# A graph layer on one core: main path started before its tests are known, lists loaded first, and no filler matmuls

## The reference

```python
msg = node_feat[src] + edge_feat
neigh = segment_sum(msg, dst, num_segments=3125)
rst = (1.0 + eps[0]) * node_feat + neigh
h = rst @ W1 + b1                       # 256 wide
h = (h - mean(h, 0)) * rsqrt(var(h, 0) + 1e-5) * gamma + beta
out = relu(h) @ W2 + b2
result = layernorm(x + out)
```

## Time and profile before

| | us |
|---|---|
| median of 3 runs | 265.76 |
| lowest, highest | 264.14, 265.84 |
| the profiled execution | 265.49 |
| its span, first to last instruction | 263.7 |
| PE, DVE, ACT, POOL busy | 240.7, 187.8, 127.9, 172.6 |

### The profile page before, as it was taken

The page is one execution under the profiler, slowest core; times in us unless marked ns, Lnnn a source line. Parts: engine busy times, 40 slices in busy tenths (PEclk is TensorE's granted clock), DMA queues, the critical chain, the costliest instruction groups (busy, mean ns, idle before and its releaser), DMA issues.

```text
span 263.7 us, 6841 instructions
## 1 busy us (share of the span) xinstructions
PE 240.7 (91%) x2205; PEld 201.5 (76%) x2205; DVE 187.8 (71%) x686; ACT 127.9 (48%) x225; POOL 172.6 (65%) x113
## 2 busy tenths in 40 slices
PE   0649689999999999999999999999999999999980
PEld 0548568889999998788888888878888879845980
DVE  2978894768789986887887878777666511288882
ACT  0406512445565665455645555544444232176794
POOL 3058888888888888888888888888888600270000
PEclk9999956999999999999999999999999999999996
DMA  5975655677789888777888787877776400000034
GB/s 156 271 232 109 138 115 100 151 153 177 192 193 209 189 196 193 171 184 189 200 186 187 183 193 176 192 165 176 156 160 155 81 0 2 4 0 0 2 114 130
DMA packets 48957, 38.11 MB, mean 145 GB/s; under 512 B 5019, under 2 KB 47947, under 8 KB 48921
## 3 DMA queue, kind: packets, MB, share of 16 engines
q1 hardware_dynamic: 32829, 30.62, 40.3%
q0 software_dynamic: 14400, 6.56, 20.8%
q10 hardware_dynamic: 1692, 0.48, 1.0%
HBM read 36.05 MB, written 1.60 MB: 143 GB/s over the span
## 4 chain that ended last, share of the span: by engine, by line
PE 79%; DVE 12%; issue 3%; ACT 2%; DVEq 2%; DMA 1%; ACTq 1%
PE ps L682 28%; PE ps L690 20%; PE ps L720 9%; PE ps L714 7%; PE ps L636 4%; PE ps L781 3%; PE ps L706 2%; DVE hit_k L952 2%; PE ps L770 2%; DVE hit_k L949 2%; DVE aggT L1022 2%; PE ps L711 1%; ACT big L561 1%; DMA x_room<-in_dst_dram 1%; PE ps L619 1%
## 5 line engine op out<-in xcount | busy, mean ns | idle before, releaser
L438 POOL DMA_INDIRECT egat<-in_x_dram,srci x100 | 163.6, 1636 | 43.1 <-issue 28.3
L524 ACT ACTIVATE big<-ps 128x500 f32 x158 | 96.7, 612 | 109.8 <-PE ps L720 83.6
L690 PEld LDWEIGHTS ps<-hit_c,ebuf 128*128 128x128 f32 x632 | 103.2, 195 | 14.9 <-DVE hit_c L920 4.7
L690 PE MATMUL ps<-hit_c,ebuf 128*128 128x20 f32 x632 | 97.3, 232 | 6.4 <-DVE hit_c L920 4.6
L1022 DVE TENSOR_TENSOR aggT<-aggT,ps 128x20 f32 x208 | 35.9, 173 | 54.9 <-PE ps L690 35.5
L682 PE MATMUL ps<-big,xN 128*128 128x114 f16 (+8 forms) x225 | 59.7, 278 | 0.4 <-ACT big L524 0.3
L682 PE MATMUL ps<-big,x_room 128*128 128x114 f16 (+8 forms) x225 | 59.6, 278 | 0.0
L682 PE MATMUL ps<-big,xr 128*128 128x114 f16 (+8 forms) x225 | 59.5, 278 | 0.0
L720 PE MATMUL ps<-hit_k,hit_l 128*128 128x400 f16 x158 | 53.2, 337 | 0.0
L714 PE MATMUL ps<-hit_k,hit_l 128*128 128x300 f16 x158 | 46.5, 294 | 0.0
L952 DVE TENSOR_TENSOR hit_k<-iota_k,key 128x800 f16<-128x800 f16 x79 | 44.9, 568 | 0.0
(11 more groups left out here) (105 smaller groups left out, 209.3 us busy)
## 6 DMA issues: line engine op xcount, KB each, us to landing
ebuf<-in_edge_attr_dram SPq DMA_DIRECT2D x79, 256.0 KB
egat<-in_edge_attr_dram SPq DMA_DIRECT2D x49, 128.0 KB
egat<-in_x_dram,srci POOLq DMA_INDIRECT x100
out_dram<-big SPq DMA_DIRECT2D x5, 256.0 KB
w_sb<-in_L_gnn_W_dram ACTq DMA_DIRECT2D x2, 128.0 KB, 6.9
out_dram<-big SPq DMA_DIRECT2D x2, 128.0 KB
x_room<-in_dst_dram SPq DMA_DIRECT2D x1, 192.0 KB
x_room<-in_src_dram ACTq DMA_DIRECT2D x1, 192.0 KB
```

The lines of the kernel that those rows point to most:

```text
L438: return nc.gpsimd.indirect_dma_start(to, None, x[:, :], bass.IndirectOffsetOnAxis(ap=ix, axis=0), compute_op=op)
L524: nc.scalar.activation(cnt[:, :, bass.ds(lows[m % LOADS], WIN)], ps[:, m % BANKS_C, 0:KEYS].rearrange("p (t n) -> p t n", n=WIN), ACT.Copy ...
L690: last = nc.tensor.matmul(ps[:, SUMS + w % BANKS_S, 0:WIN], rows_v[:, j * D:(j + 1) * D], hits_v, start=(j == 0), stop=(j == ROWS - 1))
```

## The change

- **One path first.** The branch ahead of the loop is gone. The loop always runs; the tests are cut in seven steps that DVE does at windows 21, 24, ... 39 of its loop, PE shares the result behind window 42, the flag is set at index 46, and block 2's multiply waits for it. The branch (`If(flag == 0)`) stands near the end: on ACT ahead of the hidden stores, on DVE ahead of the last sums (with the batch statistics inside), on PE behind four of the eight matmuls on x + b2, on SP and POOL behind their loops. The general path is now the `Else`, loads lists and x again, and does the whole sum anew. `firsts` is clamped (two operations on DVE) so that a wrong input can't write outside.
- **Order of the head.** SP waits for both lists before it issues any edge, then chunks, slots and x in seven pieces by turns, then the weights (from ACT's queue). Key rows come before low bits; rel, sources and carry are copied by ACT; clearing `cnt`'s end is moved ahead of the lists' arrival. The constants made by POOL are smaller.
- **Constants.** `FROM_B` 4 to 5 (counts b 400 to 375 columns, its hit table 400 to 376), the last two blocks (8 and 2 groups) are one of 10, `MARGIN` 36 to 30, x split every third window (`SPREAD`) and transposed two tiles a window (`X_RATE`), `KEEP` 24 to 0. A helper `fill` is there, with all its counts at zero.

By the planner's arithmetic the block sizes were 114, 180, 256, 376, 468, 466, 332, 120, 110 columns, and become 120, 180, 256, 376, 468, 466, 332, 218. The first gathered windows were 6, 9, 12, 14, 18, and become 7, 10, 13, 16, 18. Block 0 is multiplied from window 13 on both before and after.

```diff
-FROM_B = 4
-WIN_B = WIN - FROM_B
+FROM_B = 5
+WIN_B = 15
-BLOCKS_C = (10, 12, 17, 25, 31, 31, 22, 8, 2)
+BLOCKS_C = (10, 12, 17, 25, 31, 31, 22, 10)
-MARGIN = 36
+MARGIN = 30
-SPREAD = 2
-X_RATE = 3
+SPREAD = 3
+X_RATE = 2
-KEEP = 24
-KEEP_FROM = 7
+KEEP = 0
+KEEP_FROM = 0
-KEPT = 810
+KEPT = 0
-TURN = 1660
+TURN = 0
-GATHER_FIRST = 16000
+GATHER_FIRST = 19000
+TEST_STEP = 3
+FILL_HEAD = 0
+FILL_KEY = 0
+FILL_LO = 0
+FILL_CARRY = 0
+FILLS = ()
...
+        LAST_TILE = [max(n for n in range(NT) if X_TILES[n][0] == i) for i in range(NB)]
+        SCALE_AT = [next(m for m in range(GC) if C_AT[m] >= n // X_RATE) for n in LAST_TILE]
+        TEST_F = 1
+        W_TESTS = READY[0] + 8
+        W_WORST = W_TESTS + 7 * TEST_STEP
+        W_SHARED = W_WORST + 4
...
-            for n in range(SLOTS):
+            sp.wait_ge(dst_loaded, 80)
+            sp.wait_ge(src_loaded, 64)
+            chunk(0)
+            x_piece(X_ORDER[0])
+            slot(0)
+            x_piece(X_ORDER[1])
+            chunk(1)
+            x_piece(X_ORDER[2])
+            slot(1)
...
+            chunk(3)
+            x_piece(X_ORDER[6])
+            for n in range(3, SLOTS):
                 slot(n)
-                if n < CHUNKS:
-                    chunk(n)
+            sp.dma_start(w1_sb[:, :], w1).then_inc(weights_loaded, 16)
...
             nc.scalar.activation(srcf, srcq, ACT.Copy).then_inc(src_rows_made, 1)
+            act.wait_ge(rel_turned, 1)
+            nc.scalar.activation(spread(rel[:, :]), banked(2), ACT.Copy).then_inc(rel_made, 1)
...
+            act.wait_ge(src_turned, 1)
+            nc.scalar.activation(spread(srci[:, :]), banked(7)[:, QC:Q, :], ACT.Copy).then_inc(sources_made, 1)
...
+                for i in range(NB):
+                    if SCALE_AT[i] == m:
+                        scale_x(i, x_turned, x_scaled)
...
+                    if u == 0 and f == TEST_F + 1:
+                        pe.wait_ge(path_known, 1)
...
-                    if KEEP_FROM <= m < KEEP:
-                        for n in range(2):
-                            nc.tensor.matmul(ps[:, m % BANKS_C, 0:KEYS_B], iota_k[:, 0:P], iota_k[:, 0:KEYS_B], start=True,
-                                             stop=True, skip_group_check=True)
...
+            pe.wait_ge(x_b2_added, 1)
+            preload(0, 4)
+            pe.wait_ge(path_known, 1)
+            flag = pe.value_load(wide[0:1, 0:1], min_val=0, max_val=1)
+            with pe.If(flag == 0):
+                pe.wait_ge(hidden_stored, NB * HH)
+                preload(4, len(ROW_PIECES))
+                products()
...
+            nc.vector.memset(cnt[:, :, CNT - SPARE:CNT], 0.0).then_inc(spare_zeroed, 1)
...
+                if w == W_TESTS:
+                    find_most(0)
+                if w == W_TESTS + TEST_STEP:
+                    find_most(2)
...
+                if w == W_SHARED:
+                    dve.wait_ge(worst_shared, 1)
+                    nc.vector.tensor_scalar(wide[:, :], ps[:, ACC + (TEST_F + 1) % 2, 0:1], 0.5, None,
+                                            ALU.is_gt).then_inc(wide_made, 1)
...
+            dve.wait_ge(path_known, 1)
             flag = dve.value_load(wide[0:1, 0:1], min_val=0, max_val=1)
+            with dve.If(flag == 0):
+                last_sums()
+                hidden_stats(hidden_stored)
+            with dve.Else():
+                last_sums()
```

More of the change, by code:

```diff
@@ L507, in _ @@
+            act.wait_ge(weights_loaded, 80)
             act.wait_ge(path_known, 1)
             flag = act.value_load(wide[0:1, 0:1], min_val=0, max_val=1)
-            with act.If(flag != 0):
+            with act.If(flag == 0):
+                store(hidden_made, hidden_stored)
+            with act.Else():
+                store(hidden_made, hidden_stored)
                 for i in range(NB):
[L511 to L535, removed]
+                    scale_x(i, gen_x_turned, gen_x_scaled)
+                store(gen_hidden_made, gen_hidden_stored)
@@ L572, in _, with fill @@
         def _(pe):
+            def fill(bank, n):
+                for _ in range(n):
+                    nc.tensor.matmul(ps[:, bank, 0:KEYS_B], iota_b[:, 0:P], iota_b[:, 0:KEYS_B], start=True, stop=True,
+                                     skip_group_check=True)
+            pe.wait_ge(filler_made, 1)
+            fill(0, FILL_HEAD)
             pe.wait_ge(ident_made, 1)
-            pe.wait_ge(row_loaded, 32)
-            pe.wait_ge(constants_made, 2)
-            nc.tensor.matmul(ps[:, 7, 0:D + 1], ones[0:1, :], row[0:1, :], start=True, stop=True).then_inc(b2_shared, 1)
             def turn(bank, v, n):
@@ L591, in _ @@
             turn(2, lambda k: rel_v[:, k // ROWS, k % ROWS, :], HJ).then_inc(rel_turned, 1)
+            pe.wait_ge(row_loaded, 32)
+            pe.wait_ge(constants_made, 2)
+            nc.tensor.matmul(ps[:, 6, 0:D + 1], ones[0:1, :], row[0:1, :], start=True, stop=True).then_inc(b2_shared, 1)
+            fill(0, FILL_KEY)
+            pe.wait_ge(key_rows_made, 2)
+            turn(3, lambda k: key_v[:, k, :], HJ).then_inc(key_turned, 1)
+            fill(0, FILL_LO)
             pe.wait_ge(place_rows_made, 2)
@@ new lines, in _, with preload @@
+            multiply(F - 1, 0, UNITS)
+            pe.wait_ge(counts_stored, GC)
+            pe.wait_ge(weights_loaded, 80)
+            hidden(0, NB * HH, sums_complete, hidden_made, hidden_stored)
+            def preload(a0, a1):
+                for a in range(a0, a1):
+                    t0, t1 = ROW_PIECES[a]
+                    r = rows_of(t1 - 1)
+                    nc.tensor.matmul(ps[0:r, (a + 4) % 8, 0:(t1 - t0) * D], ident[0:r, 0:r],
+                                     xN[0:r, t0:t1, :].rearrange("p t d -> p (t d)"), start=True, stop=False,
+                                     skip_group_check=True)
@@ L785, in _ @@
+                hidden(0, NB * HH, gen_sums_complete, gen_hidden_made, gen_hidden_stored)
+                pe.wait_ge(gen_hidden_stored, NB * HH)
+                preload(0, len(ROW_PIECES))
+                products()
         @block.vector
@@ new lines, in _, with find_most, find_least @@
+            dve.wait_ge(key_turned, 1)
+            key_d = key[:, :, :].rearrange("p (q k) two -> p q k two", k=HJ)
+            for a in range(2):
+                last = nc.vector.tensor_copy(key_d[:, :, :, a], banked(3)[:, 0:QC, :])
+            last.then_inc(key_made, 1)
+            rel_t = relq.rearrange("q (t c) -> q t c", c=P)
+            def find_most(i):
+                nc.vector.tensor_reduce(most[:, i:i + 2], rel_t[:, i:i + 2, :], AX_X, ALU.max).then_inc(tests_made, 1)
+            def find_least(i):
+                nc.vector.tensor_reduce(least[:, i:i + 2], rel_t[:, i:i + 2, :], AX_X, ALU.min).then_inc(tests_made, 1)
```

822 lines of the change are left out of this document (451 added, 371 removed).

## The result

The changed kernel takes 272.5 us (median of 4 runs, 271.9 to 275.9) beside 265.8 for the kernel before; the ratio is 1.026, with an interval of 1.020 to 1.032. The forecast was 259.0. The profiled execution took 271.9, its span is 270.0.

The account below looks back on a forecast made before the run. TensorE (PE) bounds most of the span, VectorE (DVE) the head and, with PE at low clock, windows 0 to about 20. Gains 3.2 + 2.1 + 1.6 = 6.9 from 265.5 give 258.6, forecast 259.0 us; range 255.0 to 264.0.

Parts of the forecast that it names:

- a low stretch as long as that of before, 10.2 us: Windows 13 to 20: clock falls once, costing 2.8, say 3.0 us; leaves a gain of 3.2 us at index 21.
- fourth rival: Windows 13 to 45: clock stays low while DVE feeds PE, 50 us instead of 31, total 275 and more; chance 0.08.
- a rise ahead of window 13: Loop indices 1 to 12: priced at full clock with DVE setting the pace, 17.3 us, ending at 33.4.
- second rival: Whole run: clock never falls after its first rise, 3.0 us less, 256.0; chance 0.17.
- The head: Before the loop: tests, branch and copies leave DVE; first x split at 16.0 instead of 19.92, 3.9 us gained.
- x in pieces, SP's wait: Load queue: SP waits for both lists, x comes in seven pieces; costed at nothing, else stalls up to 1 us each.
- Windows 0 to 20, set by DVE: Early loop: DVE sets the pace, reaching 41.6 instead of 47.80; 6.2 us gained if the clock is full.
- Windows 21 to 45: Loop: DVE's 19.8 us plus 3.0 of tests make 22.8 against 24.9 before; gain 2.1 us.
- Counts b: Windows 46 to 207: 400 to 375 columns saves 0.0104 us a window, 1.6 us, of which 1.2 counted.
- The 0.4 of the merged block: Block multiplies: one block fewer, 75 matmuls of 110 columns took 3.65 us before; gain 0.4 us.
- The tail and the jump: After the loop: last block 7.0 us; DVE's extra jump, at most 1.0 us, covered by 1.55 us of slack; cost 0.
- The gather: Hundred gathers start at 11 and end near 205, 9 us slack; rival that it sets the end, chance 0.03.

Follow-up runs that it names:

- e4: Changed kernel with three transposes of x a window instead of two; 270.1 us, ratio 1.015 to the kernel before.
- e3: Kernel before without its 34 constant matmuls, all else as it was; 273.8 us, ratio 1.026.
- e5: Changed kernel plus 16 constant matmuls in the head and two in each counted window 0 to 23; 259.9 us, ratio 0.975.
- e9: Changed kernel plus 16 head fillers, counts b of 400 columns, two fillers in counted windows 0 to 11 only; median 256.1 us, ratio 0.967.
- e6: e5 with counts b of 400 columns again (FROM_B = 4, WIN_B = 16) instead of 375; 259.1 us, ratio 0.974 to the kernel before.
- e2: Changed kernel plus two constant matmuls in every counted window from 0 to 23, none in the head; 263.8 us.
- e10: Changed kernel plus 16 head fillers, counts b of 400 columns, one filler in each counted window 0 to 23; 261.9 us, ratio 0.990.
- e12: e10 with an x split at every second window (SPREAD = 2) instead of every third; 262.1 us, ratio 0.979.
- e11: Changed kernel plus 16 head fillers and counts b of 400 columns, no fillers in the loop; 270.3 us, ratio 1.020.

## Why the prediction was wrong

**The step that failed** is the length of the low stretch. I took "a low stretch as long as that of before, 10.2 us", and set the fourth rival aside with "at the low clock PE is the bound and full, which is how the clock rose at 44.1". PE was full there, but full with fillers in it: one of the pairs of the earlier trace rows stands at 43.61, just ahead of the rise. Full of the loop's own work alone, it stayed low: in the changed kernel for 27.5 us without an idle moment, in e4 for 30.7 and in e3 for 37.5 us in all. I had read the busy share of that stretch and not what filled it, although the change took away just that.

The forecast also took for granted a rise ahead of window 13. It did not come, and that cost nothing by itself: the split at index 13 starts at 33.0 us, against 33.4 forecast.

The fourth rival is nearest to what came, in the length of the stretch and not in its reason: it had the clock low as long as DVE feeds PE, and it stayed low with PE full. Its price a microsecond fits. From window 13 on (33.4 by the forecast) the changed kernel is low for 34.9 us; at 0.38 each that is 13.3. With 9.9 gained at a full clock and the 2.1 of the columns below, 265.8 - 9.9 + 13.3 + 2.1 gives 271.3, against 272.5 measured. Its worked case of 50 us for windows 13 to 45 was too long: windows 12 to 44 took 45.6, because the clock came back at 68.3. Its chance, 0.08, was too small, and the range left it out. The second rival (it never falls) needs fillers: e5, low for 3.4 us, takes 259.9 against 256.0, and three of e9's five executions took 256.0 to 256.1.

**The head: right.** First x split at 15.6 against 16.0. On the chain key is copied from 8.75 and hits_c follows at 9.67. ACT's table load starts at 4.71, not at 7.45 as in the earlier trace rows, since the weights left its queue.

```profile
8.75 0.07 DVE key L973
...
9.16 0.51 DVE key L973
...
9.67 0.20 DVE hit_c L1017
```

**x in pieces, SP's wait: right.** No DMA is among what PE waited for between 8 and 75 us.

**Windows 0 to 20, set by DVE: right at a full clock, and on the long side.** In e5 the sum of window 19 comes at 39.9, against 41.6; the price of 1.3 us for the wait for the last x_scaled was 1.5:

```profile
32.72 0.21 PE L757 MATMUL ps<-big,xN 128*128 128x120 f16 x1 [1.49 <-ACT aggT L591]
```

**Windows 21 to 45: not tested as forecast.** 22.8 us were forecast, with 3.0 of tests. e5 takes 24.4 with fillers and the tests hidden. The changed kernel takes 32.4, 22.2 of them at the low clock. No profile has these windows at a full clock without fillers.

**Counts b: wrong sign.** I took 25/400 of the matmul's time off, 1.2 us, and nothing in the rows said that time goes by columns for a view of 25 runs of 15. Measured is 0.8 us more from window 44 on (e5 beside e6). With the 1.2 not gained that is 2.0 of the 2.1 missing there. The 0.4 of the merged block can't be told from scatter: with 400 columns the merged block's kernels take 184.1 to 184.7 us from window 52 on, the kernel before 184.8 and e3 184.6.

Two slips in the working changed nothing: the parts given for a counted window (0.26, 0.03, 0.13, 0.16, 0.23) add up to 0.81 and not 0.84, and the earlier trace rows have 0.18 for counts b, not 0.16 or 0.17.

**The tail and the jump: right.** The chain of the changed kernel, columns as in the earlier trace rows, and relu's first output beside the earlier trace rows:

```profile
227.51 7.01 PE ps L757 x75
234.52 10.72 PE ps L737 x28
...
250.81 9.14 PE ps L870 x80
```
```profile
248.86 0.43 DVE L1246 TENSOR_SCALAR big<-big 128x512 f32<-128x512 f32 x1
```

The last block takes 7.0 us; relu is ready 1.52 us ahead of the products, 1.55 before. The jump cost nothing that shows.

**The gather: right that it doesn't bind.** Against the earlier trace rows it starts 4.2 us sooner, but the last starts at 208.9 and not near 205; PE waits for none.

```profile
L523 POOL DMA_INDIRECT egat<-in_x_dram,srci x100: 1543/1560/4007, 11.4 to 208.9; - x100
```

## What to carry to other kernels

A matmul on a constant can be part of the speed of the real ones. Before taking it out, look at the stretch in which the clock rose and ask what PE ran there, instruction by instruction, not how busy it was; then price the low clock for as long as the loop would last without it. Read the clock from the length of one matmul at several places as well as from the clock row. The version to keep is e6, the change with 16 fillers in the head, two in each counted window to 23 and counts of 400 columns: 0.974 of the kernel before (0.971 to 0.976), with little scatter (258.3 to 259.3 us). e9 has the lower median but took 267 us in two of five executions. Execute a kernel whose clock moves several times before you compare: one profile shows one of its courses.

## What the runs showed of the hardware

- PE without an idle moment and yet at 1.2 GHz: 27.5 us in the changed kernel, 30.7 in e9. The Trainium skill (TensorE: Matmul & The Clock Gate, Part 1: The HAM clock gate) has activity release the throttle; these rows disagree if activity is read as the busy share of the profile. What in the fillers makes the difference stays open.
- In the loop the clock fell with no idle piece of PE over 1.8 us ahead of it: the longest is 1.43 us before, 1.77 in e3, 1.30 in e4. An idle piece of 1.49 us at the same matmul was followed by a fall in e2, e9 and e10, and by none in e5 and e6.
- In the five kernels with no fillers at that place (changed, e3, e4, e9, e11) the clock came back 5.9 to 7.8 us after PE began matmuls of 180 columns in place of 120 or 114.
- The clock record begins with its first change, so a kernel that starts low and rises late shows a granted clock of 1.00: the changed kernel's mean is 0.993, with 68 us low.
- Matmuls of 375 columns in 25 runs of 15 have records of 339 ns where 400 in 25 runs of 16 have 329; the next matmul starts 171 and 168 ns after them.
- Some kernels have two times: e9 takes 256 or 267 us, e12 between 259 and 268, and beside them the kernel before took 269.6 or 269.7 us in three of eight executions and 263.5 to 265.7 in five.
